# Gate and up projection swap accumulator banks in a fused attention and feed-forward kernel

## The reference

```
xn = _layernorm(x, axis=-1)
# attention
q = (xn @ Wq.T).reshape(b, t, 8, 64)
kv_latent = xn @ Wkv_down.T
k = (kv_latent @ Wk_up.T).reshape(b, t, 8, 64)
v = (kv_latent @ Wv_up.T).reshape(b, t, 8, 64)
attn = softmax(einsum('bqhd,bkhd->bhqk', q, k) * 64 ** -0.5)
att = einsum('bhqk,bkhd->bqhd', attn, v).reshape(b, t, 512) @ Wo.T
# feed-forward, inner width 704; fp4_linear(x, w) quantizes x and w in blocks of 16
gate = fp4_linear(xn, w_gate)
y = fp4_linear(xn, w_up)
h = silu(gate) * y
out = x + att + fp4_linear(h, w_down)
```

## Time and profile before

| | |
|---|---|
| median of 3 runs | 1498.85 us (1498.58 to 1499.34) |
| profiled execution | 1497.88 us |
| its span, first to last instruction | 1496.1 us |
| mean granted TensorE clock | 0.984 of full speed |
| TensorE, GpSimd, VectorE, ScalarE busy | 93%, 81%, 80%, 48% |
| one block in the steady part | 86.8 us |

### The profile page before, as it was taken

How to read it: one execution, slowest core, us unless ns; L and a number is a source line. 1 busy time by engine, 2 the same in 40 slices (tenths; PEclk the granted TensorE clock), 3 DMA queues, 4 the chain that set the end, 5 groups by cost and what they waited for, 6 DMA issues and landing times.

```text
span 1496.1 us, 25492 instructions
## 1 busy us (share of the span) xinstructions
PE 1383.9 (93%) x7910; PEld 1021.1 (68%) x7910; DVE 1189.6 (80%) x2472; ACT 716.9 (48%) x1574; POOL 1213.7 (81%) x1336
## 2 busy tenths in 40 slices
PE   1489999999999999999999999999999999999996
PEld 1356677776767777676777677677767767676675
DVE  7677978888787888878888887888888788867662
ACT  3444545445454544545454454545454554545441
POOL 7648888879788887978888788879878887986773
PEclk9689999999999999999999999999999999999998
DMA  4032222222223222222222222222212322221220
GB/s 125 0 78 56 62 79 69 61 65 71 72 58 78 71 65 58 72 75 60 72 72 67 55 72 79 64 65 72 74 50 70 82 63 62 65 68 49 59 58 29
DMA packets 73557, 98.07 MB, mean 66 GB/s; under 512 B 12752, under 2 KB 40144, under 8 KB 73424
## 3 DMA queue, kind: packets, MB, share of 16 engines
q1 hardware_dynamic: 73424, 96.45, 24.4%
HBM read 37.16 MB, written 8.65 MB: 31 GB/s over the span
## 4 chain that ended last, share of the span: by engine, by line
PE 63%; DVE 17%; POOL 11%; issue 4%; ACT 3%; DMA 1%; SPq 0%; POOLq 0%; DVEq 0%; ACTq 0%
PE m L871 30%; PE po L1032 12%; PE mx L971 5%; PE st L999 5%; PE st L1000 5%; POOL key_sum L518 4%; DVE row_max L723 4%; PE m L1046 2%; DVE inv_den L794 2%; DVE hid L768 2%; DVE hid L764 2%; DVE xn L819 1%; PE m L1124 1%; PE m L983 1%; POOL h_norm L537 1%
## 5 line engine op out<-in xcount | busy, mean ns | idle before, releaser
L608 ACT ACTIVATE probs<-st 128x512 f32<-128x512 f32 x512 | 284.0, 594 | 334.3 <-PE st L1000 334.3
L518 POOL TENSOR_TENSOR key_sum<-key_sum,probs 128x512 f32<-128x512 f32 x256 | 329.1, 1285 | 38.0 <-ACT probs L608 1.7
L723 DVE TENSOR_REDUCE row_max<-mx 128x1 f32<-128x512 f32 x512 | 322.9, 672 | 1.2 <-PE mx L971 0.6
L1032 PE MATMUL po<-probs,lat_tok 128*64 128x512 f32 x1024 | 233.8, 598 | 0.0
L999 PE MATMUL st<-q_hi,lat 128*128 128x512 f32 x512 | 216.9, 424 | 0.5 <-ACT probs L608 0.5
L1000 PE MATMUL st<-q_lo,lat 65*128 65x512 f32 x512 | 203.1, 397 | 0.0
L971 PE MATMUL mx<-lat,q_hi 128*128 128x512 f32 x512 | 176.0, 418 | 11.4 <-DVE row_max L723 4.3
L871 PE MATMUL m<-wgu_hi,xt_hi 128*128 128x352 f32 x512 | 168.8, 330 | 3.5 <-DVE lat_tok L851 1.7
L616 ACT ACTIVATE hid<-m 128x352 f32<-128x352 f32 x128 | 59.5, 465 | 233.7 <-PE m L871 233.7
L871 PE MATMUL m<-wgu_hi,xt_lo 128*128 128x352 f32 x512 | 166.3, 325 | 0.0
L871 PE MATMUL m<-wgu_lo,xt_hi 128*128 128x352 f32 x512 | 166.1, 324 | 0.0
(11 more groups left out here) (179 smaller groups left out, 3347.4 us busy)
## 6 DMA issues: line engine op xcount, KB each, us to landing
q_hi<-qp_hi SPq DMA_DIRECT2D x256, 128.0 KB, 2.3
q_lo<-qp_lo SPq DMA_DIRECT2D x128, 128.0 KB, 2.4
inv_b<-inv_rows SPq DMA_DIRECT2D x128, 128.0 KB, 2.8
x_in<-in_L_attn_x_dram SPq DMA_DIRECT2D x64, 128.0 KB, 2.3
acc<-in_L_attn_x_dram SPq DMA_DIRECT2D x64, 128.0 KB, 2.1
out_dram<-acc SPq DMA_DIRECT2D x32, 256.0 KB, 2.9
q_lo<-neg_max SPq DMA_DIRECT2D x128, 2.0 KB
inv_rows<-inv_den SPq DMA_DIRECT2D x64, 4.0 KB
```

Source lines behind the costliest of these rows:

```text
L518: pool.tensor_tensor(total, first, last, ALU.add).then_inc(sum_step, 1)
L608: act.activation(probs[:, t.c % 2, kc, :], st[kc % 2][:, :], ACT.Exp).then_inc(exp_done, 1)
L723: dve.tensor_reduce(row_max[:, u.c % 2, qc:qc + 1], mx[qc % 2][:, :], AX.X, ALU.max).then_inc(mx_taken, 1)
L1032: last = pe.matmul(po[v * R:(v + 1) * R, :], lat_tok[:, s.c % 2, kc, 0:R], probs[:, v, kc, :], start=(kc == 0), stop=(kc == CH - 1))
```

## The change

Gate and up change banks. The gate goes to `m1`, where also the queries, the latents and their transposes go; the up projection goes to `m0`, with the down product and the output projection. Each wait for the feed-forward reader of a bank is exchanged with it: who writes `m1` waits for `silu_done`, who writes `m0` for `hid_done`. The order of the two is now turned round (up first) in slots that follow the latents and their transposes, slots 5 and 7, and no longer in those that follow the output projection, slots 3 and 4.

```diff
-                    act.activation(hid[:, t.c % 2, :], m0[:, 0:HALF], ACT.Tanh, scale=0.5).then_inc(tanh_done, 1)
+                    act.activation(hid[:, t.c % 2, :], m1[:, 0:HALF], ACT.Tanh, scale=0.5).then_inc(tanh_done, 1)
...
-                    dve.scalar_tensor_tensor(h, h, 1.0, m0[:, 0:HALF], ALU.add, ALU.mult).then_inc(silu_done, 1)
+                    dve.scalar_tensor_tensor(h, h, 1.0, m1[:, 0:HALF], ALU.add, ALU.mult).then_inc(silu_done, 1)
...
-                    dve.tensor_tensor(h, h, m1[:, 0:HALF], ALU.mult).then_inc(hid_done, 1)
+                    dve.tensor_tensor(h, h, m0[:, 0:HALF], ALU.mult).then_inc(hid_done, 1)
...
             def m0_free(t):
...
-                    pe.wait_ge(silu_done, t.n(1, 1))
+                    pe.wait_ge(hid_done, t.n(1, 1))
...
             def m1_free(t):
...
-                    pe.wait_ge(hid_done, t.n(1, 1))
+                    pe.wait_ge(silu_done, t.n(1, 1))
...
             def gate(t):
                 if t.within(SLOTS):
+                    m1_free(t.plus(-1))
+                    into_hidden(t, m1, 0, gate_psum)
+            def up(t):
+                if t.within(SLOTS):
                     m0_free(t.plus(-1))
-                    into_hidden(t, m0, 0, gate_psum)
-            def up(t):
-                if t.within(SLOTS):
-                    m1_free(t.plus(-1))
-                    into_hidden(t, m1, I, up_psum)
+                    into_hidden(t, m0, I, up_psum)
...
-                if wov_half(t.plus(-1)) is None:
+                if lat_seq(t.plus(-1)) is None and ltok_seq(t.plus(-1)) is None:
                     gate(t)
                     up(t)
```

More of the change, by code:

```diff
@@ L1011, in gate @@
                 if t.within(SLOTS):
-                    m0_free(t.plus(-1))
-                    into_hidden(t, m0, 0, gate_psum)
+                    m1_free(t.plus(-1))
+                    into_hidden(t, m1, 0, gate_psum)
             def up(t):
                 if t.within(SLOTS):
-                    m1_free(t.plus(-1))
-                    into_hidden(t, m1, I, up_psum)
+                    m0_free(t.plus(-1))
+                    into_hidden(t, m0, I, up_psum)
             def weigh(t):
```

## The result

The changed kernel takes 1475.61 us in the median of 4 runs (1473.53 to 1478.39), beside 1498.95 us (1498.58 to 1499.34) for the kernel before on the same chip. The ratio is 0.9847, 95% interval 0.9833 to 0.9860, so 1.5% faster. The profiled execution took 1476.33 us with a span of 1474.5 us, at a granted clock of 0.985 of full speed.

A forecast was written before the change was run, and what follows sets the result against it. TensorE, 93% busy, was taken to bound the kernel through its stops at the queries, with GpSimd also on the path. Savings of 1.33 us a block, 19.9 us in all, gave 1478.0, plus 1.0 to the median: 1479 us, range 1471 to 1488.

The forecast's parts named there:

- Slot 3: Gate first lets silu end before TensorE is ready, so the queries' whole stop goes: 1.10 us a block gained.
- Slot 1: Queries wait for silu instead of hid and start 0.63 us earlier, of which only 0.12 us a block is gained.
- the cap: In slot 2 the softmax sums need GpSimd's last key sum; 0.26 less a 0.14 hand-over leaves 0.12 us.
- Slot 5: Gate goes second, yet queries start at 752.37 instead of 752.48: 0.11 us a block gained.
- Slot 7: Gate second starts the queries 0.08 us later, covered by what remains of slot 1's stop: counted as nothing.
- the wait for the down product: In slot 7 VectorE waits 0.90 us for it, which was to cover silu coming 0.70 us later.
- slower rival: In slot 7 VectorE, 0.70 us late, is blocked by two more GpSimd key sums: 1514 us; 5%.
- GpSimd's stop in slot 4: GpSimd's wait for TensorE at the attention output's low part, 3.74 us, was to shrink to near 2.4.
- Block: A block of eight slots was to last 85.5 us, 1.33 us less than 86.8.
- Key sum is no stop: Slot 1's 0.63 us pass slot 2 whole, 0.51 us more in each of 13 blocks: 1472 us; 12%.
- VectorE late in slot 3: VectorE reaches silu 1.1 us later than reckoned, so half of slot 3's 1.10 is left: 1487 us; 12%.
- Nothing moves: Another engine sets the pace of the block and TensorE just waits elsewhere: time stays at 1499 us; 5%.

The follow-up runs named there:

- e1: Changed kernel, but in all odd slots the queries wait for hid_done again instead of silu_done; 1491.54 us, ratio 0.9961.
- e4: Kernel before with its banks and waits, but gate always first, slots 3 and 4 too; 1501.59 us, ratio 1.0018.
- e2: Changed kernel, but in slot 1 alone the queries wait for hid_done again; 1479.94 us, ratio 0.9873.
- e5: Changed kernel, but GpSimd takes its first key sum ahead of the token chunk's step that waits for VectorE; 1489.29 us, ratio 0.9944.
- e9: Changed kernel with GpSimd's key sums made on half of the columns only, so softmax sums are wrong; 1464.60 us, ratio 0.9773.
- e11: Changed kernel with queries behind the second key scores in slots 5 and 7, and GpSimd's first key sum ahead in slot 6 alone; 1468.64 us, ratio 0.9799.

## Why the prediction was right

Forecast 1479 (1471 to 1488), measured 1475.61. Point by point, with the forecast's own terms:

- **Slot 3**, 1.10 us. From the turn of slot 3 to the turn of slot 4 the block shrank by 1.09 (13.06 to 11.97); the stretch from `on_lo` of slot 2 to that of slot 4, with slot 1's share, shrank by 1.22 (24.47 to 23.25), which is the forecast's 1.10 and 0.12. Silu was free in time (with its hand-over at 717.11, against the 717.71 at which TensorE was ready: 0.60 of margin where I had 0.5 to 0.61). `e1` shows that the order does it, `e4` that the order without the banks does not.
- **Slot 1**, 0.12 us of 0.63. The mechanism is as told: the stop is cut to 0.26, and the wait for the key sum appears in 9 of 13 blocks with 0.36 to 0.46 us. By `e2` slot 1 is worth 0.23, so the term was too small by 0.1. The stop of 0.92 us that the forecast read in one block was there in seven of thirteen; in four others most of it stood at the row-max scores. I had placed the cap on the one hand-over from the key sum. Behind it stands a larger fact: GpSimd sets the stretch from slot 6 to slot 2, by its own work and by what it holds up on VectorE (`e5`, `e9`, `e11`).
- **Slot 5**, 0.11 us. The stretch from slot 4 to slot 6 shrank by 0.17. The gap gives 0.09 of it. The rest is that the twelve matmuls of gate and up in slot 6 start every 0.160 us instead of 0.166. I have no cause for it.
- **Slot 7**, nothing. The gap grew by 0.10 (forecast 0.08) and the stretch by 0.06. VectorE's silu moved late, as told, but what covered it was not the wait for the down product, as the forecast's sum had it: in slot 7 that wait is 0.98 us in the mean, 0.88 before. It was the forecast's argument against the slower rival: the scale step, now later, meets the same key sum and is held for a shorter time. Slot 7 of the changed kernel, beside the earlier trace rows:

```profile
760.84 2.72 POOL L518 TENSOR_TENSOR key_sum<-key_sum,probs 128x512 f32<-128x512 f32 x2
...
762.86 0.73 DVE L697 TENSOR_SCALAR h_small<-h_small 128x22 f32<-128x22 f32 x1
...
765.73 0.42 DVE L801 TENSOR_TENSOR acc<-m,acc 128x256 f32<-128x256 f32 x1 [0.99 <-PE m L871]
```

  The step takes 0.73 us where it took 1.18, and again ends 0.03 to 0.04 behind the key sums. So the slower rival did not come. Its mechanism exists: with a key sum moved forward (`e5`, `e11`), VectorE is held ahead of `lat_tok` and the gate of slot 7 comes 0.5 to 0.9 us late.
- **GpSimd's stop in slot 4** near 2.4: 2.50. In slot 6 near 0.2: 0.18. **Block** 85.5: 85.47.
- **Rivals.** "Key sum is no stop" is out (5.2 us in 11 places, and `e2`). "VectorE late in slot 3" is out (silu ends there 0.6 us before TensorE is ready). "Nothing moves" and "slower" are out by the time.

The sum by execution was 19.9 us and came out as 21.55. Cut at the head of slot 0, it is 18.0 instead of 17.3 in the thirteen blocks, 0.75 instead of 0.5 up to the end of the first block, and 2.8 instead of 2.1 behind. The first of these excesses is not clearly the change's: at 120.7 us the two executions lay 0.02 us apart, and between 127 and 131 us the granted clock was 0.59 in the mean in that of before, with stretches at its lower level (1.2 GHz, matmuls of 352 columns 0.50 us instead of 0.33), and 1.00 in that of after, which was then 1.5 us ahead. The remaining 1.7 us to the forecast are the step from execution to median: I took +1.0 as before, and it was -0.7, which is chance. One block of the profiled execution waited at its row-max scores for the copy of the queries and lasted 86.2 us instead of 85.4. It does not account for the spread of the runs over 5 us: in later rounds the kernel before spread as much (1496.06 to 1501.61 in 15 runs).

## What to carry to other kernels

Where one of two banks comes free late, give it to the group that nobody is waiting for and write that group second. The swap pays only together with the order, so judge both in one step (alone they cost 16 and 3 us here, together they gave 23). When a stop goes, look for the engine whose stretch keeps its length to 0.1 us: here the stretch from slot 0 to slot 2 lasted 20.61 to 20.68 us in nine kernels, and of 0.6 us gained within it 0.4 was lost at its end. And do not fill an engine's idle time before asking what its neighbour does in it: GpSimd's waiting was VectorE's working time.

## What the runs showed of the hardware

- A scalar step of VectorE (from SBUF to SBUF) that starts while a GpSimd step is under way is held until that step's end: 0.17 us became 0.91 on 22 columns, 0.17 became 0.69 on 16, and 0.40 became 0.87 and 1.43 on 256. In the steady part of the changed kernel 107 steps on 22 columns end 0.03 to 0.04 us behind the GpSimd step, and 24 on 256 columns 0.15 behind. Six others, which started within 0.01 us of the GpSimd step, took their 0.17 us and were not held. The first scale step on 16 columns takes 515 ns in the mean in `e5` (its line L698) and 176 ns in the changed kernel (L697). A product with both inputs in SBUF (`rstd`, L755, one column) is held in the same way: 0.16 us free, 0.80 in the median in the 41 places where a GpSimd step was under way.
- Silu's product, which has one operand in PSUM, and the row maxima were not held up: silu took 0.50 to 0.52 us in the changed kernel in 84 places with a GpSimd step under way at its start as in 30 without, the row maxima 0.62 to 0.69 in both cases.
- A stopped stream of matmuls pays 0.11 us on top of the stop (0.51 instead of 0.40 for the first, and the next starts 0.34 behind it instead of 0.23), even where the stop itself is 0.02 us (`e1`, slot 3).
